# A fused mLSTM and mixture-of-experts kernel: the merged stage's turns all written out, and another order inside a turn

## The reference

```
x = x + tanh(g_xattn) * mlstm(layernorm(x), ctx, ctx)     # 16 heads of 64, gates from [q, k, v], ln_scale
x = x + tanh(g_ffn)   * moe(layernorm(x))                 # router over 16 experts, top 2, F = 512
                                                          # and a shared expert with F = 1024
mlstm: ig, fg = gates;  F = cumsum(log_sigmoid(fg));  D = exp(F_t - F_s + ig_s - rowmax), s <= t
       h = ((q k^T / 8) * D) v / max(|rowsum|, exp(-max));  normalised per head
moe:   each row to its two experts, silu(x Wg) * (x Wu) Wd, weighted; plus the shared expert
```

## Time and profile before

| | us |
|---|---|
| median of 3 runs | 3125.04 (3122.43 to 3129.82) |
| the profiled execution's own time | 3112.9 |
| span of the profile | 3111.3 |
| PE busy | 2968.8 (95% of the span) |
| DVE busy | 1626.6 (52%) |
| ACT busy | 1012.4 (33%) |
| POOL busy | 595.4 (19%) |
| granted TensorE clock, mean | 0.983 of full |

### The profile page before, as it was taken

How to read it: one execution, slowest core, us unless ns; L and a number is a source line. 1 busy time by engine, 2 the same in 40 slices (tenths; PEclk the granted TensorE clock), 3 DMA queues, 4 the chain that set the end, 5 groups by cost and what they waited for, 6 DMA issues and landing times.

```text
span 3111.3 us, 50365 instructions
## 1 busy us (share of the span) xinstructions
PE 2968.8 (95%) x17262; PEld 2453.0 (79%) x17263; DVE 1626.6 (52%) x3104; ACT 1012.4 (33%) x1916; POOL 595.4 (19%) x572
## 2 busy tenths in 40 slices
PE   4799999999999988999999999999999999999999
PEld 3687878787877876888888888888888888888887
DVE  4787878787788864342243324323333344444444
ACT  4444434344444422232233333322333331111111
POOL 1234333333334321000000000000000001111111
PEclk9799999999999998999999999999999999999999
DMA  6454455454554444133433333333334324444444
GB/s 192 143 166 149 143 136 172 137 150 136 168 147 143 142 151 149 62 139 138 142 135 142 136 140 142 135 142 142 135 142 142 135 81 150 147 141 159 144 138 152
DMA packets 205735, 441.92 MB, mean 142 GB/s; under 512 B 86784, under 2 KB 87680, under 8 KB 205056
## 3 DMA queue, kind: packets, MB, share of 16 engines
q1 hardware_dynamic: 110544, 333.62, 32.1%
q0 software_dynamic: 24400, 72.96, 7.2%
q10 hardware_dynamic: 70656, 33.56, 4.1%
HBM read 350.72 MB, written 107.18 MB: 147 GB/s over the span
## 4 chain that ended last, share of the span: by engine, by line
PE 59%; DVE 1%; ACT 1%; ACTq 0%; issue 0%; DVEq 0%
PE p_g_b L1568 19%; PE p_up_b L1568 19%; PE p_y_b L1556 17%; PE p_x_b L1536 3%; PE p_h_b L1543 1%; DVE w_lo L1420 1%; ACT w_hi L1363 1%; ACTq L1217 0%; ACTq L1202 0%; DVE x L1476 0%; DVE sg_b L1448 0%; DVE x L1467 0%; ACT th_b L1405 0%; DVE y_b L1478 0%; ACTq L1359 0%
## 5 line engine op out<-in xcount | busy, mean ns | idle before, releaser
L1568 PE MATMUL p_g_b<-w_hi,xt_hi_b 128*128 128x512 f32 x840 | 342.2, 407 | 16.3 <-DVE w_lo L1420 13.0
L1436 DVE TENSOR_TENSOR ht_lo_b<-p_h_b,ht_hi_b 128x512 fp32r<-128x512 f32 x105 | 72.5, 691 | 542.7 <-ACT ht_hi_b L1375 542.7
L1556 PE MATMUL p_y_b<-w_hi,ht_hi_b 128*128 128x512 f32 x840 | 339.9, 405 | 1.9 <-DVE ht_lo_b L1436 1.9
L1568 PE MATMUL p_up_b<-w_hi,xt_lo_b 128*128 128x512 f32 x840 | 331.6, 395 | 0.0
L1448 DVE SCALAR_TENSOR_TENSOR sg_b<-th_b,p_g_b 128x512 f32<-128x512 f32 x105 | 72.3, 688 | 494.6 <-ACT th_b L1405 494.6
L1568 PE MATMUL p_up_b<-w_lo,xt_hi_b 128*128 128x512 f32 x840 | 330.4, 393 | 0.0
L1568 PE MATMUL p_g_b<-w_hi,xt_lo_b 128*128 128x512 f32 x840 | 329.9, 393 | 0.0
L1556 PE MATMUL p_y_b<-w_lo,ht_hi_b 128*128 128x512 f32 x840 | 329.5, 392 | 0.0
L1568 PE MATMUL p_up_b<-w_hi,xt_hi_b 128*128 128x512 f32 x840 | 327.8, 390 | 0.0
L1568 PE MATMUL p_g_b<-w_lo,xt_hi_b 128*128 128x512 f32 x840 | 327.3, 390 | 0.0
L1556 PE MATMUL p_y_b<-w_hi,ht_lo_b 128*128 128x512 f32 x840 | 326.5, 389 | 0.0
(11 more groups left out here) (221 smaller groups left out, 5700.4 us busy)
## 6 DMA issues: line engine op xcount, KB each, us to landing
mid_y<-y_b SPq DMA_DIRECT2D x73, 512.0 KB, 3.2
stage<-mid_g_row SPq DMA_DIRECT2D x64, 512.0 KB, 5.1
stage<-in_eg SPq DMA_DIRECT2D x16, 2048.0 KB, 9.1
stage<-in_eu SPq DMA_DIRECT2D x16, 2048.0 KB, 15.3
stage<-in_ed SPq DMA_DIRECT2D x16, 2048.0 KB, 19.5
mid_y<-in_x SPq DMA_DIRECT2D x34, 512.0 KB, 8.9
stage<-in_x SPq DMA_DIRECT2D x32, 512.0 KB
stage<-in_ctx_t ACTq DMA_DIRECT2D x32, 512.0 KB, 7.9
```

The costliest lines, as they stand in the source:

```text
L1436: nc.vector.tensor_tensor(ht_lo[:, :, :], p_h[:, :, :], ht_hi[:, :, :].bitcast(f32), ALU.subtract).then_inc(ht_rdy, 1)
L1556: last = nc.tensor.matmul(p_y[n][:, :], a[:, k, :], b[:, GUP + k, w], start=(k == 0 and m == 0), stop=(k == FE // P - 1 and m == 2))
L1568: mm = nc.tensor.matmul(out[:, :], a[:, k, :], w[:, k, o:o + FE], start=(k == 0 and m == 0), stop=(k == KD - 1 and m == 2))
```

## The change

`schedule` no longer makes a loop. It walks one list, `ORDER`, which is made once on the host from the parts ahead and from 35 turns, and calls each part with plain numbers. So there are no backward branches in the merged stage, and all waits are on constants. `Chain.base` and the count of DVE steps per batch go away with it.

`TURN` has another order, and R1 another distance: it was chunk t-1 in the midst of the turn, and is chunk t-2 as the second entry of the turn.

```diff
-        TURN = ("A2", "W1", "B0", "V1", "H1", "A3", "B2", "O1", "Y1", "E1", "P1", "A4", "E2", "A1", "B1", "W2", "Y2",
-                "F1", "Y3", "A5", "J1", "Y4", "N1", "W3", "B3", "A6", "L1", "N2", "T1", "W4", "S1", "Q1", "G1", "W5",
-                "A9", "F2", "B4", "A7", "A8", "E3", "G2", "R1", "G3", "C1", "F3", "G4", "X1", "G5", "Q2", "C2", "G6",
-                "E4", "W6", "Z1", "U1", "D1", "K7", "K8", "Q3")
+        TURN = ("A2", "R1", "H1", "B0", "A3", "E1", "Y1", "P1", "A4", "B2", "Y2", "E2", "V1", "B1", "Y3", "W1", "W2",
+                "T1", "A5", "Y4", "J1", "W3", "N1", "A1", "B3", "A6", "L1", "N2", "G1", "S1", "A7", "B4", "Q1", "W4",
+                "A9", "E3", "G2", "A8", "F1", "O1", "F2", "G3", "G4", "C1", "F3", "C2", "X1", "Q2", "G5", "W5", "E4",
+                "Z1", "G6", "K7", "K8", "U1", "Q3", "W6", "D1")
...
-        SHIFTED = {"U1": -2, "D1": -1, "K7": -2, "K8": -2}
+        SHIFTED = {"R1": -2, "K7": -2, "K8": -2, "U1": -2, "D1": -1}
...
-        def schedule(eng, chain, stages, fori):
...
-            with fori(1, B - 1) as b:
...
+        ORDER = list(AHEAD)
+        for turn in range(NCH + 3):
+            items = [(name[0], int(name[1:]), turn + offset(name[0], name[1:])) for name in TURN]
+            ORDER += [item for item in items if 0 <= item[2] < NCH and item not in AHEAD]
+
+        def schedule(stages):
+
+            for stage, part, c in ORDER:
                 if stage in stages:
-                    stages[stage](part, 0, j)
...
+                    stages[stage](part, c // CPB, c % CPB)
...
-        self.eng.wait_ge(self.sem, self.base + self.n)
+        self.eng.wait_ge(self.sem, self.n)
```

More of the change, by code:

```diff
@@ L31 @@
 NEG = -3.0e38
-DVE_PER_BATCH = 147
 SLOTS = 4
@@ L54, in __init__ @@
     def __init__(self, eng, sem):
-        self.eng, self.sem, self.base, self.n = eng, sem, 0, 0
+        self.eng, self.sem, self.n = eng, sem, 0
     def step(self, ins):
@@ L61, in settle @@
     def settle(self):
-        self.eng.wait_ge(self.sem, self.base + self.n)
+        self.eng.wait_ge(self.sem, self.n)
     def settle_apart(self, past):
-        ge_apart(self.eng, past, (self.sem, self.base + self.n))
+        ge_apart(self.eng, past, (self.sem, self.n))
     def link(self, ins):
@@ L225, in offset @@
             return SHIFTED.get(f"{stage}{part}", OFFSET[stage])
-        def schedule(eng, chain, stages, fori):
[L229 to L238, removed]
-                if stage in stages:
-                    stages[stage](part, 0, j)
-            for j in range(CPB):
-                turn(0, j)
-            before = chain.n if chain else 0
-            with fori(1, B - 1) as b:
[L245 to L254, removed]
+        ORDER = list(AHEAD)
[4 more added lines that the diff above has]
+            for stage, part, c in ORDER:
+                if stage in stages:
+                    stages[stage](part, c // CPB, c % CPB)
         def heads(g):
@@ L290, in decays_at_router @@
             return capped((CPB - 2) * b + (2, 2, 3, 4)[j], (CPB - 2) * B)
-        tr_turn = [(stage, int(part)) for stage, part in TURN if stage + part in ("Q2", "Q3", "N1", "N2", "H1")]
-        tr_ahead = [(stage, part, j) for stage, part, j in AHEAD if stage == "Q" and part > 1]
+        turned = [item for item in ORDER if f"{item[0]}{item[1]}" in ("Q2", "Q3", "N1", "N2", "H1")]
         def tr_before(stage, part, b, j):
[L297 to L313, removed]
+            n = turned.index((stage, part, b * CPB + j))
+            return tr_done(turned[n - 1][0], turned[n - 1][1], *divmod(turned[n - 1][2], CPB)) if n else None
         def tr_done(stage, part, b, j):
@@ L448, in stage_p @@
                     load_scales()
-            schedule(sp, None, {"P": stage_p, "X": stage_x, "R": stage_r, "W": stage_w, "A": stage_a, "D": stage_d,
-                                "F": stage_f, "E": stage_e, "J": stage_j, "V": stage_v, "Z": stage_z}, sp.Fori)
+            schedule({"P": stage_p, "X": stage_x, "R": stage_r, "W": stage_w, "A": stage_a, "D": stage_d,
+                                "F": stage_f, "E": stage_e, "J": stage_j, "V": stage_v, "Z": stage_z})
             sp.wait_ge(xn_out, 16 * NCH)
@@ L526, in stage_e @@
                             in_=tok[:, j % 2:j % 2 + 1], in_offset=None).then_inc(done, 16)
-            schedule(pool, None, {"L": stage_l, "A": stage_a, "C": stage_c, "D": stage_d, "E": stage_e}, pool.Fori)
+            schedule({"L": stage_l, "A": stage_a, "C": stage_c, "D": stage_d, "E": stage_e})
             ge_apart(pool, past, (scat0, 16 * NCH), (scat1, 16 * NCH))
@@ L657, in stage_o @@
                         nc.scalar.activation(w_hi[:, p, :], stage[:, p, :], ACT.Copy).then_inc(gu0_hi, 1)
-            schedule(act, None, {"T": stage_t, "O": stage_o, "P": stage_p, "W": stage_w, "Q": stage_q, "F": stage_f, "N": stage_n, "A": stage_a, "B": stage_b, "C": stage_c, "E": stage_e,
-                                 "U": stage_u, "H": stage_h}, act.Fori)
+            schedule({"T": stage_t, "O": stage_o, "P": stage_p, "W": stage_w, "Q": stage_q, "F": stage_f, "N": stage_n, "A": stage_a, "B": stage_b, "C": stage_c, "E": stage_e,
+                                 "U": stage_u, "H": stage_h})
         @block.vector
@@ L948, in stage_z @@
                 count(nc.vector.tensor_scalar(starts_i[:, 1, :], starts, -1.0, None, ALU.add))
-            schedule(dve, chain, {"O": stage_o, "Z": stage_z, "W": stage_w, "L": stage_l, "Q": stage_q, "A": stage_a, "S": stage_s, "B": stage_b,
+            schedule({"O": stage_o, "Z": stage_z, "W": stage_w, "L": stage_l, "Q": stage_q, "A": stage_a, "S": stage_s, "B": stage_b,
                                   "F": stage_f, "C": stage_c, "D": stage_d, "E": stage_e, "N": stage_n, "U": stage_u, "H": stage_h,
-                                  "J": stage_j}, dve.Fori)
+                                  "J": stage_j})
             settle()
@@ L1126, in stage_z @@
                     nc.tensor.matmul(p_logit[:, 0:NE], ones[:, :], hot_acc[:, :], start=True, stop=True).then_inc(cnt_ps, 1)
-            schedule(pe, None, {"Z": stage_z, "Q": stage_q, "N": stage_n, "A": stage_a, "B": stage_b, "E": stage_e, "G": gate_up, "K": gate_up,
-                                "H": stage_h, "Y": stage_y}, pe.Fori)
+            schedule({"Z": stage_z, "Q": stage_q, "N": stage_n, "A": stage_a, "B": stage_b, "E": stage_e, "G": gate_up, "K": gate_up,
+                                "H": stage_h, "Y": stage_y})
 def expert_weights(t, e, shared_half=0):
```

1 line of the change is left out of this document (removed).

## The result

The changed kernel takes 3170.93 us (median of 4 runs, 3166.20 to 3184.77), the kernel before on the same chip 3127.43 (3122.43 to 3132.30): ratio 1.0146, interval 1.0110 to 1.0183. It is slower, as forecast, by 1.5% instead of 2.6%. The profiled execution took 3173.38 us with a span of 3171.8.

A forecast was written before the change was run, and what follows sets the result against it. PE, busy 95% of the span, bounds the kernel; its idle spots in the merged stage were the question. -27 + 68 + 34 + 4 + 3 = +82 us on 3125 gives 3207 us; own range 3160 to 3265, 8 in 10: 3100 to 3290.

The forecast's parts named there:

- Part 1: Merged stage's loop written out: the stall and slow clock at five first turns behind a jump go, -27 us.
- Rival 3: Loop stalls aren't the jump's but, for instance, code fetching; writing the loop out gains nothing, 3234 us; chance 0.05.
- Part 2: Residual rows' load R1, issued behind D1, lands at +9.3 after X1's issue; PE stalls at A5, +68.4 us.
- rival 4: R1 needs its own 3.3 us behind D1, landing at +12.6, clock falling every turn; about 3290 us; chance 0.07.
- E1 now starts at +5.27: In turn 11 of the old order, DVE's E1 starts 5.27 us after X1's issue.
- the +7.1 and +5.5 allowed: Latest E1 starts after X1's issue without PE waiting at A5: +7.1 us in turn 11, +5.5 in first turns.
- Part 3: PE's clock falls behind the new stalls at A5: 0.5 us lost per us of stall, +34 us.
- Part 4: The stage's ends: O1 behind J1 at the block's end +4 us, the start +3 us, other swaps 0.
- The start: Turns 0 and 1: F1 behind weight pieces W1 to W4 on SP, B0 no longer behind W1; +3 us.
- move within slack: Later V1, several swaps, T1 and A1 each wait for parts done earlier: 0, between -15 and +15 us.
- Rival 1: R1 isn't held up by D1, lands by +5.5; kernel gains under about +6.5; 3105 us; chance 0.24.
- Rival 2: R1 lands at about +7.8; 29 us of stall and little clock balance the loop's gain, 3125 to 3135; chance 0.08.

The follow-up runs named there:

- the first: The kernel before with only its loop written out, old order of the turn kept; 3083.00 us, ratio 0.9907.
- twelfth run: The kernel before with its loop written out and only R1 moved to the turn's second place, behind D1; 3182.54 us, ratio 1.0177.
- the fourth: The kernel before, loop and order kept, with only R1 moved to the turn's second place, behind D1; 3243.26 us, ratio 1.0431.
- third run: The changed kernel with SP's memory-to-memory copy of D1 issued right behind R1 instead of ahead of it; 3114.78 us, ratio 1.0003.
- the ninth: The kernel before with only its loop written out, run again unchanged as a measure on another chip; 3096.02 us, ratio 0.9905.
- sixth: The changed kernel with D1's copy issued behind R1, and the scales' load F1 and F2 placed as in the old order; 3108.20 us, ratio 0.9922.
- fifth: The changed kernel with R1 back in mid-turn, ahead of D1 but behind F1 on SP's queue; 3119.12 us, ratio 0.9958.
- the eighth: The kernel before with its loop written out, plus Q3's transposes put in front of K8, U1 and D1 following; 3091.96 us, ratio 0.9863.
- the second: The changed kernel with R1 (and start-up piece W5) back in mid-turn behind G2, ahead of D1 and F1; 3203.21 us, ratio 1.0293.
- the seventh experiment: The changed kernel with D1's copy issued behind R1, and H1 put back behind B0; 3152.12 us, ratio 1.0056.

## Why the prediction was right, and where its sizes were off

**The sum, as measured.** The loop: 0.9907, -29 us. The new order with R1 in time: 1.0003 - 0.9907, on one chip, +30. R1 behind D1: 1.0146 - 1.0003, +44. Together +45 or 1.46%; I had forecast +82. The way and the main mechanism were right, but that the time fell within my range of 3160 to 3265 was luck in part: the loop and R1's place alone make +15, about 3142, and the rest is a loss that I had put at nothing. (Where the first and the changed kernel are compared, it is by their ratios, for they ran on different chips.)

**Part 1** forecast -27 and got -29. Rival 3, that straight code has the stall as well, is refuted: it doesn't.

**Part 2** had the mechanism and the place. I forecast R1's landing at +9.3, with D1's; the median is +9.28. The figure is right by luck, for its make-up isn't: D1 lands at +5.91, sooner than before, and R1 not with it but 2.3 us behind in the median of the turns. Neither my rule (with D1) nor rival 4's (3.3 us behind D1) holds turn by turn: the lag goes from 0.45 to 6.4 us. Nor is it the same elsewhere: 1.8 us in the median of the twelfth run, 0.9 in that of the fourth. What sets the lag isn't shown. What failed in the sum is the stall that follows from it, 68.4 us. PE's idle time at A5 came to 57.9 us in the turns that I counted, and 15.9 of these are there with R1 in time, so R1 accounts for 42. The step that was mis-sized is "E1 now starts at +5.27", with the +7.1 and +5.5 allowed from it: I took the old order's free time for the new one's. In the new order DVE is ready for E1 only at +8.04 (third run), so R1 at +9.3 makes it 1.3 us later, not 4. The 0.15 us that I put between `rows` and PE is right: 0.14 in the turn shown above. Where the old order is kept, the same landing gives 58.2 and 72.6 us.

**Part 3,** the clock, +34. Windows over turns 3 to 29 of the changed kernel and of the third experiment's, A2 to A2:

```profile
97.24:1094.62 997.38, 908.90 (x7077) 753.16 (x7078) 786.97 (x1804) 404.84 (x951) 351.16 (x236) 0.95 0.47 139
```

```profile
96.27:1028.33 932.06, 883.90 (x7076) 732.03 (x7077) 790.62 (x1804) 403.32 (x951) 348.32 (x235) 0.99 0.49 149
```

The same work on PE takes 25.0 us longer, at a mean granted clock of 0.95 against 0.99. The difference of the stretches, 65.3 us, is 42 of stall and 25 of clock to within 2 us. It is more than the 44 of the medians; the two executions ran on chips on which the kernel before differs by 14 us. So 0.6 us a us of stall, where I took 0.5, if none of the 25 is the chips' own difference. On one chip, the twelfth run against the ninth, the same turns take 94.2 us longer, 42.7 of it PE's busy time, and the idle time at A5 grows by 56.6 us: 0.75. The share was somewhat low, on a base that was too large.

**Part 4.** O1 behind J1: +4 forecast. PE's wait at the block's end grew by 3.2 us, but from the last A2 to the experts the changed kernel takes 142.3 us against 141.3, 1.0 more. The start: +3 forecast; turn 3 begins at 97.2 instead of 100.4, 3 us sooner, and turn 4 at 135.0 instead of 139.1. That the swaps "move within slack", "0, between -15 and +15 in all", is the step that failed most: it is +30. Its bound was narrower than its own row, too, for 0.9 us a turn in 27 turns is 24. I tested each moved part against the slack of PE, and never asked which instructions of DVE and POOL would come to lie beside each other. Of the +30, between 11 and 25 are F1's and F2's (sixth against fifth and third). The turns' head on PE isn't it. How the rest divides between A1 and T1, O1 and the small swaps isn't settled. That `absf` costs DVE 43 us more, and 24 less when F1 is early, is measured; how much of that reaches PE isn't.

**The rivals.** Rival 1's landing is what the third experiment made true, and its time was not 3105 but the kernel before's, for the same missing 30 us. Rival 2's time was too low by its own terms: -20 and 29 of stall make +9, 3134, before any clock. Rival 1's rule "under about +6.5 the kernel gains" was wrong: with +5.1 it doesn't. Rival 4's landing, +12.6, didn't come in the median, but the turn shown above, +13.58, is such a case. The prediction weighed two rules of the Trainium skill, page "DMA: Bandwidth & Descriptors", section "Queues, rings and completion order". The trace agrees with the second, that a semaphore increment lands only after earlier writes: issued behind D1, R1's lands behind D1's in 26 of 26 turns; issued ahead of it, in 0 of 26. Whether R1's data landed sooner than its semaphore no trace shows.

**Both kernels are beaten** by the loop alone, 0.9907 and 0.9905, and by the eighth, 0.9863; whether the eighth beats the loop alone isn't shown.

## What to carry to other kernels

A load that is needed soon should not be issued on one queue behind a large transfer that nobody waits for in the meantime; swapping the two costs nothing and was worth 1.4% here. When an order is changed, write down for each queue who now stands behind every waiting instruction and who consumes what is moved, since the second and the seventh experiment failed on exactly that. Don't carry the slack of one order over to another, and check which DVE instructions come to lie beside POOL's.

## What the runs showed of the hardware

- A DVE instruction on 16x128 elements took 2.47 us beside a POOL product of 2.36 us, and 0.28 us when the two did not overlap. In the third kernel it ended 0.15 us behind the product in each of the 25 turns in which they met.
- A load of 512 KB landed 4.7 us after its issue when it stood ahead of a copy of 512 KB from memory to memory on the same queue, and 8.2 us after it when it stood 0.6 us behind. The copy landed at +9.10 when it went second, +5.91 when it went first, and nobody waits for it before the block's end.
- A loop with five jumps back cost 29 us in all, 5.8 for each jump with the clock behind it. The page "Advanced Engine Details and Errata" of the Trainium skill, section "Control Flow Timing", which the prediction cited, gives 0.05 to 0.11 us for a branch; what else at the loop's turn took the time no run shows, and the measured 5.8 us decides.
- The same move of one load cost 2.7% in straight code (1.0177 against 0.9905) and 4.3% in the loop. The 0.5 us later issue there is seen; that it is the whole reason isn't shown.
